# Two-pass engine programs, a shorter TensorE loop, and other cuts of the last transfers in a four-layer kernel bound by its weights

## The chip, the cores and the metric

The kernel runs on one core of a Trainium2 chip. The metric is the device time of one execution in microseconds (us). Times of single instructions and transfers come from one profiled execution, counted from the first instruction of the span.

## The reference

An image x of 16 channels, 64 by 64, passes four layers, all in float32:

```
x = L0(x, style)    # blur statistics: (x - mean(x)) / std(x) * std(style) + mean(style), 13 x 13 Gaussian
x = L1(x, weights)  # patch and window attention, below
x = L2(x, w1, b1, w2, b2)  # conv3x3, relu, conv3x3, + x
x = L3(x, weights)  # the same as L1, with weights of its own
```

L1 and L3 are the bulk. The image is cut into 64 patches of 8 x 8 x 16 = 1024 values, and into 4 windows of 32 x 32 x 16 = 16384 values:

```
fl = LN(patches); pw = softmax(q k^T)  with q, k = fl @ Wqk_p      # 1024 x 2048
pf = merge(pw @ v + dwconv(v)) @ Wout_p  with v = fl @ Wv_p        # two of 1024 x 1024
ww = softmax(q k^T) of the 4 windows, with q, k = LN(pooled) @ Wqk_w   # 1024 x 2048
wv = heads(LN(windows) @ Wv_w)                                     # 16384 x 1024
wf = merge(nondiag(ww) @ wv + dwconv(wv)) @ Wout_w                 # 1024 x 16384
out = diag(ww) * pf + wf + x
```

Wv_w and Wout_w have 64 MB each, in each of the two layers.

## The kernel before, in words

**Weights.** All weights pass through SBUF once. A *slot* is 128 partitions x 2048 values (1 MB), a *half* is 8 slots (8 MB), and the buffer `ring` holds two halves, `extra` a quarter (4 slots). SyncE issues every transfer (`load_half`, L271; `load_end`, L260). Before it overwrites slots it waits on `slots_used`, which TensorE raises by one for each slot that it has read. TensorE waits on `half_landed` before the first slot of a half. The very last half is split into six pieces, `LAST_PIECES` (L58): each is a range of columns (0 to 384 is "wide", 384 to 512 "narrow") and a range of heads, and has a semaphore of its own (L306).

**TensorE's program** (`block.tensor`). L341 to L376 compute layer L0 and turn small tables. Then one hardware loop `pe.Fori(0, 2) as L` (L378) does both attention layers with the same code: statistics, Wqk_p and Wv_p (L404, L413), Wqk_w (L421), Wout_p (L469), then a loop of 4 turns over Wv_w (L485), then a loop over Wout_w (L524). A turn of that loop is two *groups* of 8 slots: `group(L, i, g)` makes 32 matmuls (L512) into `bank[6 + g]`, ScalarE copies the bank to SBUF (`copy_group`, L653), `turn_group` transposes it (L323), and VectorE adds it to the image (`add_group`, L932). The loop runs 4 turns in the first layer and `TURNS - L` = 3 in the second. Between the layers `pe.If(L < 1)` does the two convolutions of L2.

**The tail.** The fourth turn of the second layer is written out behind the layer loop, since its second group is the half in six pieces. Its order is this:

```
group(1, TURNS - 1, 0)
last_piece(0)
turn_group(4 * TURNS - 1, 0)
last_piece(1)
```

The image is then turned into rows (8 transposes) and copied to `out_rows` by VectorE and ScalarE; the last 4 rows of each window take another way: the residual is added in PSUM by 16 small matmuls against the identity (L572, L574), between pieces. Pieces 2 to 5 follow. SyncE stores the rows in two transfers of 28 rows each (L310), the wide part of the last rows (L312) and at the end the narrow part (L314).

**The other programs.** ScalarE and VectorE are unrolled over the two layers, with small loops inside for the turns. GpSimd clears buffers and makes two products per layer. All engines run free of each other but for semaphores. `image_ready` (VectorE, L731) tells that L0 is done; SyncE waits for it before it issues the second half of the ring (L271), because L0's buffers lie there.

Of the kernel before, what the change touches and what calls it, by code (L numbers as in the profile page):

```python
# [22 lines left out]
P = 128  # L23
# [34 lines left out]
LAST_PIECES = ((0, WIDE, 0, 4), (0, WIDE, 4, 6), (0, WIDE, 6, 8), (WIDE, BANK, 0, 4), (WIDE, BANK, 4, 7), (WIDE, BANK, 7, 8))  # L58
# [61 lines left out]
def build(nc, images, blurs, const, const_low, window_gains, small, l2w, ends, halves, last, out, windows_last):  # L120
    with ExitStack() as ctx, ExitStack() as engines:
# [121 lines left out]
        LAST = WIN - 4  # L243

# [4 lines left out]
        def stores_landed(sp):  # L249
            sp.wait_ge(rows_stored, 16 * 3)  # L250
            sp.wait_ge(last_stored, 16)
# [6 lines left out]
        def _(sp):  # L258
# [50 lines left out]
            for wy in range(2):  # L309
                sp.dma_start(out[wy], out_rows[wy * WIN:wy * WIN + LAST, :]).then_inc(rows_stored, 16)  # L310
# [7 lines left out]
        def _(pe):  # L318
# [19 lines left out]
            pe.wait_ge(blurs_landed, 16)  # L338
            pe.wait_ge(images_landed, 16)
            for x8 in range(NX8):  # L340
                m = mm(bank[x8 // 4][:, x8 % 4 * P:x8 % 4 * P + P], l0_in[:, x8, :], cc("blur_y"), start=True, stop=True)  # L341
            m.then_inc(blurred_y, 1)
            pe.wait_ge(squared, 1)
            for x8 in range(NX8):
                m = mm(bank[2 + x8 // 4][:, x8 % 4 * P:x8 % 4 * P + P], l0_sq[:, x8, :], cc("blur_y"), start=True, stop=True)
            m.then_inc(blurred_y2, 1)
            pe.wait_ge(blocks_built, 1)
            for sq, img, dst in ((0, 0, 5), (1, 0, 7), (0, 1, 6), (1, 1, 0)):
                pe.wait_ge(blur_copied, 1)
                if sq:  # L350
                    pe.wait_ge(blur2_copied, 2)
                mid = l0_blur[:, sq, :].rearrange("p (x i y) -> p i x y", i=2, y=IMG)[:, img]
                field = bank[dst][:, :].rearrange("p (x y) -> p x y", y=IMG)
                mm(field, blocks_x[:, 0, :], mid, start=True, stop=False)  # L354
                mm(field[:, 0:1], blocks_x[:, 1, :], mid[:, 0:1], start=False, stop=False)
                mm(field[:, 7:8], blocks_x[:, 2, :], mid[:, 7:8], start=False, stop=False)
                mm(field[:, 0:7], blocks_x[:, 3, :], mid[:, 1:8], start=False, stop=False)
                mm(field[:, 1:8], blocks_x[:, 4, :], mid[:, 0:7], start=False, stop=True).then_inc(field_ready, 1)

            pe.wait_ge(ident_built, 2)  # L360
            for x8 in range(NX8):
                m = turn(bank[4][:, x8 * IMG:x8 * IMG + IMG], l0_in[0:IMG, x8, :], rows=IMG)
            m.then_inc(field_ready, 1)

            pe.wait_ge(const_landed, 16 * 2)
            pe.wait_ge(gains_landed, 16)
            for i in range(4):
                turn(bank[2][:, i * P:(i + 1) * P], area[0][:, i * P:(i + 1) * P])
            pe.wait_ge(small_landed, 16)  # L370
            turn(bank[3][:, 0:2 * N_SMALL], area[1][0:2 * N_SMALL, 0:P], rows=2 * N_SMALL).then_inc(vec_turned, 1)

            pe.wait_ge(l0_var, 1)
            pe.wait_ge(pads_zeroed, 1)
            pe.wait_ge(l2_landed, 16)
            mm(bank[7][:, 0:N_L2], cc("repeat", C), l2[:, :], start=True, stop=True).then_inc(l2_repeated, 1)  # L376

            with pe.Fori(0, 2) as L:  # L378

                pe.wait_ge(image_ready, L + 1)  # L380
                mm(bank[0][:, :], ones, pixels, start=True, stop=True).then_inc(sums, 1)  # L381
                pe.wait_ge(py_ready, L + 1)
                pe.wait_ge(vec_copied, 1)
                for q in range(4):
                    m = mm(bank[3][32 * q:32 * q + 32, 0:32], cc("pool"), py[:, :, :].rearrange("p y (w q) -> p q y w", q=4)[:, q],
                           start=True, stop=True)
                m.then_inc(pool_ready, 1)
                pe.wait_ge(sq_ready, L + 1)
                mm(bank[0][:, :], ones, area[1][:, :], start=True, stop=True).then_inc(var_sums, 1)  # L389
                pe.wait_ge(pooled_copied, L + 1)  # L390
                mm(bank[2][:, 0:32], ones, pooled[:, :, :, :].rearrange("p a b c -> p (a b c)"), start=True, stop=True).then_inc(pool_sums, 1)
                pe.wait_ge(sqw_ready, L + 1)
                mm(bank[1][:, :], ones, area[3][:, :], start=True, stop=True).then_inc(var_sums, 1)
                pe.wait_ge(sqp_ready, L + 1)
                mm(bank[3][:, 128:160], ones, pooled_q[:, :, :].rearrange("p a b -> p (a b)"), start=True, stop=True).then_inc(var_sums, 1)

                fl = a3(0, TOK)
                pe.wait_ge(fl_ready, L + 1)
                for s in range(S_QKP, S_VP):
                    first_there(L, s)  # L400
                    w = slot_of(s).rearrange("p (m h b d) -> p m b h d", m=2, b=2, d=P)
# [608 lines left out]
```

## Time and profile before

| | us |
|---|---|
| median of 3 runs | 747.84 |
| lowest, highest | 747.6, 748.36 |
| the profiled execution | 747.63 |
| its span, first to last instruction | 746.4 |
| TensorE busy (matmul) | 436.4 (58%) |
| VectorE busy | 91.5 (12%) |
| ScalarE busy | 38.2 (5%) |
| bytes moved | 320.45 MB, 429 GB/s on average |
| mean granted TensorE clock | 0.78 of full |

### The profile page before, as it was taken

Reading aid. Unit: us, or ns where it says so; the run is one execution under the profiler, and the core shown is the slowest. Engines: PE = TensorE matmul, PEld = TensorE weight load, DVE = VectorE, ACT = ScalarE, POOL = GpSimd, SP = SyncE. Lnnn points to the kernel's source line nnn. Section 1 sums busy time; section 2 is a strip of 40 time slices with the busy share of each in tenths; the row PEclk is TensorE's granted clock in tenths of the full one; section 3 lists DMA queues with packets and bytes.
Section 4 is the critical chain, followed back from the end, with each engine's and each line's share of the span. In section 5 each row is a group of like instructions: output and inputs, shape, how many; then the busy total and the mean of one; then the engine's idle time right before and its main releaser. Section 6 shows DMA issues by size and latency. Waiting matters only on the chain.

```text
span 746.4 us, 6667 instructions
## 1 busy us (share of the span) xinstructions
PE 436.4 (58%) x2895; PEld 129.9 (17%) x2895; DVE 91.5 (12%) x254; ACT 38.2 (5%) x80; POOL 9.3 (1%) x21
## 2 busy tenths in 40 slices
PE   7699944444445454454586989445444454544548
PEld 5333200000001111111122332000000011111113
DVE  2765200000002000000005161000000020000000
ACT  2211100000000000000001111000000000000000
POOL 2100000000000000000001000000000000000000
PEclk9689977777767777777788899876776777777779
DMA  9999999999999999999999999999999999999998
GB/s 394 447 394 436 454 415 439 436 443 418 436 446 418 439 433 443 421 432 446 418 439 436 417 434 443 446 418 432 443 432 432 432 446 418 432 443 432 432 415 347
DMA packets 7923, 320.45 MB, mean 429 GB/s; under 512 B 1049, under 2 KB 1585, under 8 KB 2153
## 3 DMA queue, kind: packets, MB, share of 16 engines
q1 hardware_dynamic: 7913, 320.31, 99.5%
q8 instruction: 7, 0.11, 0.1%
q14 instruction: 3, 0.02, 0.0%
HBM read 319.82 MB, written 0.49 MB: 429 GB/s over the span
## 4 chain that ended last, share of the span: by engine, by line
DMA 64%; PE 32%; DVE 3%; ACT 1%; issue 0%; SPq 0%; DVEq 0%; ACTq 0%
DMA ring<-halves 60%; PE bank L485 10%; PE bank L512 9%; PE bank L404 4%; DMA ring<-last 4%; PE bank L421 2%; PE bank L413 2%; PE bank L536 1%; PE bank L341 1%; PE bank L323 0%; PE bank L389 0%; DMA cst<-blurs 0%; DVE ring L722 0%; PE bank L381 0%; PE bank L354 0%
## 5 line engine op out<-in xcount | busy, mean ns | idle before, releaser
L485 PE MATMUL bank<-ring,stage 128*4 128x512 f32 x1024 | 141.4, 714 | 141.1 <-DMA ring<-halves 141.1
L512 PE MATMUL bank<-ring,wf_t 128*32 128x512 f32 x960 | 137.9, 739 | 127.3 <-DMA ring<-halves 127.3
L512 PEld LDWEIGHTS bank<-ring,wf_t 128*32 128x32 f32 x960 | 33.7, 133 | 221.1 <-DMA ring<-halves 121.0
L485 PEld LDWEIGHTS bank<-ring,stage 128*4 128x4 f32 x1024 | 27.0, 97 | 255.1 <-DMA ring<-halves 154.1
L932 DVE TENSOR_TENSOR image<-bank,image 128x32 f32 (+1 forms) x30 | 5.1, 193 | 277.6 <-PE bank L323 277.6
L897 DVE COPY wv_t<-bank 128x32 f32<-128x32 f32 x2 | 0.4, 192 | 287.1 <-PE bank L323 287.1
L323 PE MATMUL bank<-ident,area 128*128 128x128 f32 (+1 forms) x117 | 18.3, 284 | 12.3 <-ACT area L653 11.1
L653 ACT COPY area<-bank 128x512 f32<-128x512 f32 x15 | 8.8, 586 | 281.2 <-PE bank L512 281.2
L404 PE MATMUL bank<-extra,area 128*64 128x512 f32 x64 | 18.2, 734 | 3.3 <-DVE area L806 3.3
L469 PE MATMUL bank<-extra,area 128*64 128x512 f32 x64 | 17.6, 712 | 2.0 <-DVE area L871 2.0
L323 PEld LDWEIGHTS bank<-ident,area 128*128 128x128 f32 (+1 forms) x117 | 12.5, 141 | 30.9 <-ACT area L653 23.8
L641 ACT COPY stage<-area 128x64 f32 x16 | 3.9, 242 | 219.3 <-PE bank L485 206.0
L421 PE MATMUL bank<-ring,pooled_n 128*32 128x512 f32 x128 | 14.6, 595 | 0.0
L847 DVE SCALAR_TENSOR_TENSOR conv_p<-v_pad,vec,conv_p 128x636 f32<-128x636 f32 x16 | 14.1, 879 | 0.4
L413 PE MATMUL bank<-ring,area 128*64 128x512 f32 x64 | 14.1, 592 | 0.0
L404 PE MATMUL bank<-ring,area 128*64 128x512 f32 x64 | 14.1, 592 | 0.0
L556 PE MATMUL bank<-ring,wf_t 128*32 128x384 f32 (+1 forms) x128 | 7.8, 382 | 0.8 <-DMA ring<-last 0.8
L404 PEld LDWEIGHTS bank<-extra,area 128*64 128x64 f32 x64 | 5.5, 171 | 14.6 <-issue 14.6
L469 PEld LDWEIGHTS bank<-extra,area 128*64 128x64 f32 x64 | 5.4, 160 | 12.7 <-issue 12.7
L687 POOL TENSOR_TENSOR area<-area,vec 128x512 f32<-128x512 f32 x2 | 2.1, 1042 | 394.1 <-DVE area L781 394.1
L341 PE MATMUL bank<-cst,ring 128*128 128x128 f32 x16 | 3.8, 431 | 4.7 <-DMA cst<-blurs 4.7
L381 PE MATMUL bank<-image,ones 128*128 128x512 f32 x4 | 3.2, 893 | 5.4 <-DVE image L731 4.6
(208 smaller groups left out, 217.0 us busy)
## 6 DMA issues: line engine op xcount, KB each, us to landing
extra<-ends SPq DMA_DIRECT2D x4, 4096.0 KB, 16.0
ring<-halves SPq DMA_DIRECT2D x4, 4096.0 KB, 20.3
ring<-last SPq DMA_DIRECT2D x1, 3072.0 KB, 22.1
ring<-last SPq DMA_DIRECT2D x2, 1536.0 KB, 25.5
ring<-last SPq DMA_DIRECT2D x1, 1024.0 KB, 28.6
ring<-last SPq DMA_DIRECT2D x1, 768.0 KB, 29.6
ring<-halves SPq DMA_DIRECT2D x33, 29.4
ring<-images SPq DMA_DIRECT2D x1, 512.0 KB, 3.6
```

What stands on the lines that cost most here:

```text
L323: return mm(dst, src, ident[0:rows, 0:rows], start=True, stop=True, is_transpose=True)
L341: m = mm(bank[x8 // 4][:, x8 % 4 * P:x8 % 4 * P + P], l0_in[:, x8, :], cc("blur_y"), start=True, stop=True)
L404: m = mm(bank[4 + m2][b * 64:b * 64 + 64, :], fl[:, s - S_QKP, :], w[:, m2, b], start=(s == S_QKP), stop=(s == S_VP - 1))
L413: m = mm(bank[6][b * 64:b * 64 + 64, :], fl[:, kt, :], w[:, t, b], start=(kt == 0), stop=(kt == KT - 1))
L421: m = mm(bank[7][32 * j:32 * j + 32, :], pooled_n[:, s - S_QKW, :], w[:, j * BANK:(j + 1) * BANK], start=(s == S_QKW), stop=(s == S_OUTP - 1))
L469: m = mm(bank[4][f * 64:f * 64 + 64, :], a3(8, TOK)[:, h, :], w[:, t, f], start=(h == 0), stop=(h == HEADS - 1))
L485: m = mm(bank[0][32 * j:32 * j + 4, :], stage[:, k // 8, at:at + 4], w[:, j], start=False, stop=False)
L512: m = mm(bank[6 + g][32 * j:32 * j + 32, :], wf_t[:, h, :], w[:, j], start=(h == 0), stop=(h == GROUP - 1))
L536: mm(dst[0:32, :], taps_edge[:, n, dy, 0, :], rows(dy, -1), start=False, stop=False)
L556: m = mm(dst, wf_t[:, h, :], w[:, h - h0, j], start=(h == 0 and c0 == 0), stop=(h == HEADS - 1))
L653: sc.copy(area[4 + g][:, :], bank[6 + g][:, :]).then_inc(group_copied, 1)
L847: then(v.scalar_tensor_tensor(conv_p[:, 0:159, 0:4], src, wt, conv_p[:, 0:159, 0:4], ALU.mult, ALU.add))
```

## The change

Five edits, in one step:

1. The whole programs of TensorE, ScalarE and VectorE stand inside `Fori(0, 2) as visit` with `If(visit > 0)`. In pass one the branch skips the body. VectorE's body is split into two such blocks (L0 and the first layer; the second layer and the end).
2. TensorE's loop over Wout_w runs 4 turns in both layers, with `If(i + L < TURNS)` around the second group. The unrolled group and turn behind the layer loop go, so that the turn stands directly behind its group.
3. The residual is added by 4 whole matmuls (stationary 128 x 128) and no longer by 16 of 32 columns.
4. The narrow pieces of the last half take 5, 2 and 1 heads and no longer 4, 3 and 1.
5. The rows are stored by 6 transfers of 15, 13, 11, 9, 7 and 1 rows and no longer by 2 of 28.

```diff
-LAST_PIECES = (..., (WIDE, BANK, 0, 4), (WIDE, BANK, 4, 7), (WIDE, BANK, 7, 8))
+LAST_PIECES = (..., (WIDE, BANK, 0, 5), (WIDE, BANK, 5, 7), (WIDE, BANK, 7, 8))
...
+        ROW_STORES = ((0, 0, 15), (0, 15, LAST), (1, 0, 11), (1, 11, 20), (1, 20, 27), (1, 27, LAST))
...
-            for wy in range(2):
-                sp.dma_start(out[wy], out_rows[wy * WIN:wy * WIN + LAST, :]).then_inc(rows_stored, 16)
+            for wy, lo, hi in ROW_STORES:
+                sp.dma_start(out[wy, lo:hi], out_rows[wy * WIN + lo:wy * WIN + hi, :]).then_inc(rows_stored, 16)
...
+            with pe.Fori(0, 2) as visit:
+                with pe.If(visit > 0):
+                    pe.wait_ge(blurs_landed, 16)
...
+                    with pe.Fori(0, 2) as L:
...
-                with pe.Fori(0, TURNS - L) as i:
-                    for g in range(2):
-                        group(L, i, g)
-                        turn_group(i * 2 + (2 * TURNS * L + g + 1), g)
+                        with pe.Fori(0, TURNS) as i:
+                            group(L, i, 0)
+                            turn_group(i * 2 + (2 * TURNS * L + 1), 0)
+                            with pe.If(i + L < TURNS):
+                                group(L, i, 1)
+                                turn_group(i * 2 + (2 * TURNS * L + 2), 1)
...
-            group(1, TURNS - 1, 0)
             last_piece(0)
-            turn_group(4 * TURNS - 1, 0)
             last_piece(1)
...
             for s8 in range(4):
-                for j in range(4):
-                    if s8 < 3:
-                        mm(bank[7][32 * j:32 * j + 32, s8 * P:s8 * P + P], residual[:, s8, j, :], ident, start=False, stop=False)
-                    else:
-                        mm(bank[6][32 * j:32 * j + 32, 0:P], residual[:, s8, j, :], ident, start=True, stop=False)
+                dst = bank[7][:, s8 * P:s8 * P + P] if s8 < 3 else bank[6][:, 0:P]
+                mm(dst, residual[:, s8].rearrange("p j w -> p (j w)"), ident, start=(s8 == 3), stop=False)
...
+            with act.Fori(0, 2) as visit:
+                with act.If(visit > 0):
...
+            with dve.Fori(0, 2) as visit:
+                with dve.If(visit > 0):
+                    first()
+                    layer(0)
+                with dve.If(visit > 0):
+                    layer(1)
```

In VectorE's program `first()` and `layer(L)` hold the old code of L0 and of one layer, unchanged.

## Rows read from the trace of the kernel before

**Rows 1.** The page: the span, and the DMA engines' busy tenths in 40 slices:
```profile
span 746.4 us, 6667 instructions
...
DMA  9999999999999999999999999999999999999998
```

**Rows 2.** The chain of waits at the end: start us, us, what:
```profile
713.72 29.57 DMA ring<-last
```

**Rows 3.** The timeline of the tail: start us, us, engine, line [idle before]:
```profile
724.40 9.22 PE L512 MATMUL bank<-ring,wf_t 128*32 128x512 f32 x64 [9.30 <-DMA ring<-halves]
733.43 2.77 PE L556 MATMUL bank<-ring,wf_t 128*32 128x384 f32 x32
...
736.13 0.66 PE L323 MATMUL bank<-ident,area 128*128 128x128 f32 x4
...
739.16 0.86 PE L572 MATMUL bank<-ident,area 128*32 128x128 f32 x24
...
739.88 0.78 SPq L310 DMA_DIRECT2D out<-extra  x2
...
740.06 2.50 PE L556 MATMUL bank<-ring,wf_t 128*32 128x384 f32 x48
...
743.34 1.08 PE L556 MATMUL bank<-ring,wf_t 128*32 128x128 f32 x32 [0.79 <-DMA ring<-last]
744.49 0.29 DVE L953 COPY area<-bank 128x128 f32<-128x128 f32 x1 [4.97 <-PE bank L556]
744.81 0.36 SPq L314 DMA_DIRECT2D windows_last<-area  x1
```

**Rows 4.** Packets that begin in 34.3 to 35.0 us, then in 36.1 to 36.2:
```profile
DMA packets 30, 0.98 MB, mean 1404 GB/s; under 512 B 15, under 2 KB 15, under 8 KB 15
...
DMA packets 2, 0.07 MB, mean 655 GB/s; under 512 B 1, under 2 KB 1, under 8 KB 1
```

**Rows 5.** Packets in 403.3:404.1, in 721.5:722.2, in 722.7:723.5, in 723.75:723.82 us:
```profile
DMA packets 12, 0.39 MB, mean 492 GB/s; under 512 B 6, under 2 KB 6, under 8 KB 6
...
DMA packets 18, 0.22 MB, mean 316 GB/s; under 512 B 9, under 2 KB 9, under 8 KB 9
...
DMA packets 20, 0.34 MB, mean 430 GB/s; under 512 B 6, under 2 KB 6, under 8 KB 6
...
DMA packets 5, 0.10 MB, mean 1404 GB/s; under 512 B 1, under 2 KB 1, under 8 KB 1
```

**Rows 6.** Instruction packets in 31:265, in 265:731, in 731:746.4 us (packets, MB, share):
```profile
q8 instruction: 5, 0.08, 0.1%
q14 instruction: 1, 0.01, 0.0%
...
q14 instruction: 2, 0.02, 0.0%
...
q8 instruction: 2, 0.03, 1.0%
```

**Rows 7.** The timeline of the start, three of its lines:
```profile
4.74 3.78 PE L341 MATMUL bank<-cst,ring 128*128 128x128 f32 x16 [4.74 <-DMA cst<-blurs]
...
27.09 1.06 DVE L731 TENSOR_TENSOR image<-ring,bank 128x512 f32<-128x512 f32 x1
...
28.17 0.35 SPq L271 DMA_DIRECT2D ring<-halves  x1
```

**Rows 8.** The list of waits: total us, times, longest:
```profile
PE bank L323 <- ACT area L653: 11.1, 14, 0.8
```

**Rows 9.** Busy time by stretch; the granted clock is the figure behind POOL:
```profile
381.00:404.90 23.90, 18.66 (x92) 5.48 (x85) 5.41 (x13) 1.91 (x3) 1.04 (x1) 0.99 1.02 440
724.40:729.16 4.76, 4.76 (x27) 1.32 (x30) 0.00 (x0) 0.00 (x0) 0.00 (x0) 0.54 0.98 418
```

**Rows 10.** L524's loop branches (min, median, max ns), and L345 in the timeline:
```profile
L524 PEldq COMPARE_BRANCH  x7: 76/208/222, 270.2 to 714.8; - x7
...
8.31 2.07 PE L345 MATMUL bank<-cst,ring 128*128 128x128 f32 x16
```

More of the change, by code:

```diff
@@ L335, in first_there @@
                     half_there(L, None, s // HALF)
[L338 to L371, printed above, removed]
@@ L723, in _, with first @@
[L723 to L732 removed]
+            def first():
+                dve.wait_ge(images_landed, 16)
+                v.tensor_tensor(l0_sq[:, :, :], l0_in[:, :, :], l0_in[:, :, :], ALU.mult).then_inc(squared, 1)
+                dve.wait_ge(blurs_landed, 16)
+                v.tensor_tensor(blocks_x[:, :, :].rearrange("p b (x c) -> p (b x) c", c=C), cc("taps_x").unsqueeze(2).to_broadcast([P, 5 * XM, C]),
+                                cc("same_c").unsqueeze(1).to_broadcast([P, 5 * XM, C]), ALU.mult).then_inc(blocks_built, 1)
+                dve.wait_ge(blurred_y2, 1)
+                v.tensor_copy(l0_blur[:, 1, BANK:2 * BANK], bank[3][:, :]).then_inc(blur2_copied, 1)
+                mean_c = area[6][:, :]
+                dve.wait_ge(mean_sq, 1)
+                then(v.tensor_copy(mean_c, bank[5][:, :]))
+                for i, (sq, fields) in enumerate(((7, 2), (0, 4))):
+                    dve.wait_ge(field_ready, fields)
+                    dve.wait_ge(mean_sq, i + 1)
+                    then(v.tensor_tensor(l0_part[:, i], bank[sq][:, :], l0_part[:, i], ALU.subtract))
+                    v.tensor_scalar(l0_part[:, i], l0_part[:, i], 0.0, None, ALU.max).then_inc(l0_var, 1)
+                    if i == 0:
+                        dve.wait_ge(l0_std, 1)
+                        then(v.tensor_scalar(l0_part[:, 0], l0_part[:, 0], EPS, None, ALU.add))
+                        then(v.reciprocal(l0_part[:, 0], l0_part[:, 0]))
+                work = l0_blur[:, 0, 0:BANK]
+                dve.wait_ge(field_ready, 5)
+                then(v.tensor_tensor(work, bank[4][:, :], mean_c, ALU.subtract))
+                then(v.tensor_tensor(work, work, l0_part[:, 0], ALU.mult))
+                dve.wait_ge(l0_std, 2)
+                then(v.scalar_tensor_tensor(work, l0_part[:, 1], EPS, work, ALU.add, ALU.mult))
+                dve.wait_ge(pads_zeroed, 1)
+                v.tensor_tensor(pixels.rearrange("p y x -> p x y"), work.rearrange("p (x y) -> p x y", y=IMG),
+                                bank[6][:, :].rearrange("p (x y) -> p x y", y=IMG), ALU.add).then_inc(image_ready, 1)
@@ L766, in softmax, with layer @@
                 return v.tensor_tensor(x, x, wide(2), ALU.mult)
-            for L in range(2):
+            def layer(L):
                 vv = vec[:, L, :]
```

508 lines of the change are left out of this document (255 added, 253 removed).

## The prediction

> **What bounds the kernel now.** The page comes first: 16 DMA engines are busy in every slice, so the transfers run without a gap [rows 1]. The chain of waits says where the span ends: a weight transfer of 29.57 us hands over at 743.34 us [rows 2]. The timeline of the tail then shows TensorE starting its last full group at 724.40 when a half lands, working almost without a break, standing idle once, for 0.79 us at 743.34, and finishing at 744.42; a 0.29 us copy and the store at 744.81 follow, and the span ends at 746.4 [rows 3]. So two things run side by side in the last 20 us: the stream of weights and a chain of TensorE work that has only 0.79 us of play.
>
> What I looked for next is why a half lands when it does. Each transfer leaves one small closing packet (under 512 B) per engine. The first half closes on 15 engines inside 34.3 to 35.0 us and on the sixteenth at 36.1, 1.1 to 1.8 us behind [rows 4]. The half that TensorE waits for at 724.40 closes on 9 engines inside 721.5 to 722.2, on 6 between 722.7 and 723.5, and on one at about 723.8; at 403.3 to 404.1, 6 engines were late [rows 5]. These counts match the instruction fetches: queue 8 (TensorE, since it is active when TensorE enters new code) five and queue 14 one by 265 us, which makes 6 late engines; two more on queue 14 by 731 us [rows 6], which make 7, so that one of them fell on an engine that was late already. A fetch pushes its engine back, and that is never made good, because the stream has no gap. The engine hit twice from queue 14 sets the landing, 723.8; the engines hit once closed by 723.5, the unhit ones by 722.2.
>
> **Part 1, the pass that only jumps.** Each of the three programs runs its loop twice; the first time every branch skips the body, so the sequencer goes to its end and back. What this can buy is that instruction blocks of the end are fetched at about 1 to 2 us, when the first work of TensorE still waits for data, until 4.74 us [rows 7], and not in the middle of the stream. VectorE and ScalarE are short: all three queue 14 fetches should move to the start. VectorE has two skipped blocks, so its pass also touches its middle. TensorE's queue 8 fetches stay for all that lies between the first block and the last: the four early ones of [rows 6]. The last block, and the one after it, move to the start. For the landing this removes the doubly late engine and leaves the once late ones: 723.8 (723.79 by the closing packet) becomes about 723.45, **-0.34 us** for the start of the tail and for each last piece. The bounds are 0 (nothing moves, or an early fetch falls on an engine that is hit again) and -1.7 us (all fetches early: 723.8 to 722.1 at best).
>
> That blocks stay once fetched is what the trace bears out: TensorE's layer loop runs all its code again from 400 us on, and queue 8 shows no packet between 265 and 731 us [rows 6]. The Trainium skill says otherwise ("Runtime: NRT & Kernel Launch", section "Instruction fetch mechanics"): the instruction memory has room for only two blocks, prefetch is purely sequential, and a taken branch to a block outside that window stalls for its fetch. By that rule pass one would gain nothing, since the end block would be dropped again; for TensorE the trace disagrees, with its zero packets over a whole second pass, and for VectorE and ScalarE, which never jump back so far, nothing here shows it.
>
> The cost of the jumps lies at the start. TensorE, VectorE and ScalarE begin 2 to 4 us later at worst (two or three fetches in a row, and the two packets of queue 8 behind 731 us took 1.0% of 16 engines' 15.4 us, 1.2 us each [rows 6]). What hides it is the queue: image_ready comes with the end of L731 at 28.15 and releases the second half at 28.17 [rows 7], while the first half still streams until 34.4 [rows 4]; from the issue of the last store to the end of its packets pass 1.6 us (744.81 to 746.4), so the cover is at least 34.4 - 28.2 - 1.6 = 4.6 us. If the cover is gone, every us beyond it lengthens the run by 1 us. I take 0.
>
> **Part 2, the shorter TensorE loop.** The last half group (group 14, counted from 0, of the second layer) goes back into the loop and is no longer unrolled behind it: 128 instructions (64 matmuls and 64 loads) and a turn less in the program, the same executed. But its order changes. Before, last_piece(0), 2.70 us, stood between the group and its turn and hid the copy by ScalarE. Now the turn follows at once and TensorE waits for the copy: 11.1 us over 14 such waits is **+0.79 us** [rows 8]. Behind the waiting turn all pieces, the row turns and the residual are queued. Then come the branches: the new If taken, the ends of both loops, the If of the convolution and the outer loop's end, five of about 0.21 us [rows 10]; they are 1.05 us beside a turn of 0.66 us, so **+0.3 us** (bounds 0 and 1.05). In all earlier turns the new If lies in the time in which TensorE waits for a half (9.30 us before 724.40) and costs nothing.
>
> **Part 3, the residual** becomes 4 whole matmuls of 128 x 128 instead of 16 of 32 columns. The 16 took 0.90 us (739.16 to 740.06) because four of them run side by side [rows 3]. Eight whole matmuls of 128 x 128 x 128 took 2.07 us at full clock [rows 10], so four take 1.04: **+0.14 us**; below, the four turns of 0.66 us [rows 3] bound it at -0.24.
>
> **Part 4, the clock.** The tail starts at the low clock, granted 0.54 on average from 724.40 to 729.16, then 1.0 [rows 9]. A start 0.34 us earlier with the same rise spends 0.34 us more at half speed: **+0.17 us**.
>
> **Part 5, heads 5, 2, 1.** Of the narrow pieces, the last two wait together today: 32 matmuls in 1.08 us from 743.34. With 5, 2, 1 only 24 of them (0.81 us) would follow that landing, a gain of 0.27 us where the stream decides. Here TensorE decides, so the same work comes in another order: 0.
>
> **Part 6, six row stores.** SyncE took 0.78 us for two stores, so six take 2.3 us [rows 3]. They begin near 740.8 and end near 743.1, with the wide store behind them; that store is not waited for before the narrow one, which comes at 744.8 or later. Hidden; gone is the cover only if the rows come 1.5 us later still. The same 56 rows are moved, behind all loads. 0.
>
> **The sum.** TensorE's chain: -0.34 (start) +0.79 (copy) +0.3 (branches) +0.14 (residual) +0.17 (clock) -0.79 (the idle time that it eats up) = +0.27 us. The stream's own end: the last piece 0.34 us earlier, and 0.27 us saved by its shape, so about -0.5 us; the later of the two counts. The profiled run took 747.63 us around its span of 746.4, so it becomes 747.9; the median of the runs lies 0.21 us above the profiled one, which gives **748.1 us**. About 0.2%, or 1.5 us, is what a measurement of this kernel can tell from no change: 746.34 to 749.34 counts as the same.
>
> **The rivals.** (a) *The stream still decides*: copy and branches are covered, or the clock rises earlier. For it: the once idle 0.79 us; against it: nothing stands between group and turn any more. 747.84 - 0.5 = 747.3 us. Chance 0.20. (b) *All fetches move to the start*, TensorE's middle ones too. For it: the pass touches all programs; against it: TensorE's pass jumps over its middle. The tail starts 1.7 us earlier at 722.7, and the sum becomes -1.7 +0.79 +0.3 +0.14 +0.17 to 0.85 -0.79, so -1.1 to -0.4, 746.7 to 747.4; with branches and residual at their lower bounds 746.1. Chance 0.17, of which 0.12 faster by over 0.2%. (c) *The jump does not do what it says*: the early blocks are dropped and fetched again, and the late engine stays at 723.8. That is the rule of the skill named above; by rows it costs the 0.34 and gives back the 0.17: 748.3 us. Chance 0.15. (d) *Slower: the clock falls in the new gap.* The 0.8 us wait at 733.3 has 11 us of TensorE work behind it, and if the granted clock drops to 0.5 there for one more stretch like the first (4.8 us), half of that, 2.4 us, is added: 750.5 us. It decides from the point at which the grant falls before 744. Against it: the stretch from 381 us, which holds waits of the same length, was granted 0.99 [rows 9]. Chance 0.06. (e) *Slower at the start:* the jumps take more than the 4.6 us of cover, say 7: 750.5 us. Chance 0.04. The forecast keeps 0.38.
>
> **How the numbers follow.** The likeliest case spans 747.3 to 748.9 (branches and residual at their bounds, the clock's rise some us earlier or later). The range takes in (a), (c) and most of (b), and part of the slower ones: 746.4 to 749.3. Faster by over 0.2%: 0.14. Slower: (d) and (e), 0.10. Same: 0.76.
>
> **What would show it.** Part 1: the queue 14 packets of the span stand before 5 us, queue 8 has four in mid-stream and none behind 731; the half that starts the tail closes on no engine later than the once hit ones. Part 2: a wait of 0.8 us for ScalarE's copy between group and turn, and the first piece 0.2 to 0.4 us behind the turn. Part 3: four matmuls in 0.7 to 1.04 us. Part 5: no idle time of TensorE before the last pieces. Wrong it is if TensorE still idles for the stream at the end, if the last landing moves by more than 0.5 us, or if the second half is issued behind 33 us.

## The result and the profile after

| | before | after |
|---|---|---|
| median of 16 runs, us | 747.81 | 749.29 |
| lowest run | 747.5 | 747.78 |
| highest run (one disturbed run of before left out) | 748.36 | 750.58 |
| the profiled execution | 747.63 | 748.88 |
| its span | 746.4 | 747.6 |

The changed kernel is slower: the ratio is 1.002 with the interval 1.0012 to 1.0027, and the medians differ by +1.48 us. I had forecast +0.26. The changed kernel also scatters more, over 2.8 us where before spans 0.9 in these 16 runs. In the three sets of runs beside the experiments, the kernel before spans 1.0, 1.0 and 2.5 us, the last with a single run at 750.03.

The profiled execution shows +1.25 us of it, so that is what can be followed line by line. The first view is the timeline of the tail of the changed kernel (start us, us, engine, line, what, [idle before]); it answers to [rows 3].

```profile
725.59 8.47 PE L515 MATMUL bank<-ring,wf_t 128*32 128x512 f32 x64 [8.31 <-DMA ring<-halves]
...
734.13 0.58 ACT L655 COPY area<-bank 128x512 f32<-128x512 f32 x1 [17.56 <-PE bank L515]
...
734.77 0.66 PE L324 MATMUL bank<-ident,area 128*128 128x128 f32 x4 [0.72 <-ACT area L655]
...
736.15 4.08 PE L561 MATMUL bank<-ring,wf_t 128*32 128x384 f32 x48 [0.73 <-issue]
...
741.09 1.06 PE L574 MATMUL bank<-ident,area 128*128 128x128 f32 x8
...
742.08 3.58 PE L561 MATMUL bank<-ring,wf_t 128*32 128x384 f32 x80
...
745.73 0.29 DVE L958 COPY area<-bank 128x128 f32<-128x128 f32 x1 [4.19 <-PE bank L561]
746.04 0.35 SPq L315 DMA_DIRECT2D windows_last<-area  x1
```

The tail starts at 725.59 and not at 724.40: +1.19 us. From there to the end of the last matmul it takes 20.07 us (725.59 to 742.08 + 3.58 = 745.66), before 20.02 us (724.40 to 744.42). So the whole loss of this execution stands ahead of the tail, and inside the tail the gains and losses cancel out.

What delays the start is seen in the closing packets. These are counts of packets of the changed kernel in 722.1 to 722.8, in 723.6 to 724.25 and in 725.05 to 725.1 us; they answer to the last three lines of [rows 5].

```profile
DMA packets 15, 0.24 MB, mean 339 GB/s; under 512 B 7, under 2 KB 7, under 8 KB 7
...
DMA packets 21, 0.32 MB, mean 492 GB/s; under 512 B 8, under 2 KB 8, under 8 KB 8
...
DMA packets 5, 0.10 MB, mean 1966 GB/s; under 512 B 1, under 2 KB 1, under 8 KB 1
```

Seven DMA engines close early, eight are late, and one closes at 725.07, 2.90 us behind the first (722.17). Before, nine were early, six late, and the last came at 723.79, 2.20 us behind the first (721.60). The landing is 1.28 us later. Of that, 0.70 is a wider spread, and 0.57 is that even the first engine closes later. Most of this is there 35 us into the run already. These are the closing packets of the very first half in the changed kernel, counted in 34.8 to 35.4, 36.2 to 36.7 and 37.7 to 37.8 us; they answer to [rows 4].

```profile
DMA packets 24, 0.80 MB, mean 1338 GB/s; under 512 B 11, under 2 KB 11, under 8 KB 11
...
DMA packets 8, 0.26 MB, mean 524 GB/s; under 512 B 4, under 2 KB 4, under 8 KB 4
...
DMA packets 3, 0.13 MB, mean 1311 GB/s; under 512 B 1, under 2 KB 1, under 8 KB 1
```

The first engine closes at 34.88 (before 34.38), the last at 37.73, 2.85 us behind it (before 1.77 behind). From there to the tail the largest distance stays between 2.79 and 2.91 us: the fetches of the middle set other engines back, none of them as far.

The instruction packets say where the late engines come from. Stretches of the changed kernel: 0 to 12, 12 to 265.5, then 731 to 747.6 us (between 265.5 and 731 there is none), against [rows 6].

```profile
q8 instruction: 2, 0.03, 1.0%
q14 instruction: 3, 0.02, 0.5%
...
q8 instruction: 5, 0.08, 0.1%
...
q8 instruction: 1, 0.02, 0.4%
```

The three fetches of queue 14 (VectorE and ScalarE) did move out of the middle. But TensorE's five are still there, at 35, 69, 83, 115 and 265 us (before 32, 66, 81, 112 and 264), and two more are made at the start. And "the start" is not 1 to 2 us: the five early fetches begin at 3.65, 3.76, 3.94, 10.37 and 10.60 us, when the weight transfers run already. In all, ten fetches lie in the stream ahead of the tail's half where there were eight.

The start itself, TensorE's taken branch and the start of its work, then the issue of the second half; they answer to [rows 7]. The first line is the listing of one source line (min, median, max ns of two branches, when), the others are of the timeline.

```profile
L340 PEldq COMPARE_BRANCH  x2: 77/2618/5159, 1.1 to 6.9; - x2
...
3.63 1.58 SPq L267 DMA_DIRECT2D cst<-const_low  x1
...
7.11 3.76 PE L344 MATMUL bank<-cst,ring 128*128 128x128 f32 x16 [7.11 <-DMA cst<-blurs]
...
29.78 1.05 DVE L735 TENSOR_TENSOR image<-ring,bank 128x512 f32<-128x512 f32 x1
...
30.86 0.35 SPq L272 DMA_DIRECT2D ring<-halves  x1
```

One branch to code that is not there took 5.16 us. TensorE's first matmul comes at 7.11 and not at 4.74, the image at 30.83 and not at 28.15, and the second half is issued at 30.86 and not at 28.17 us. The first half still streams then: its first engine is done at 34.88, the last at 37.73. So this 2.7 us stays hidden. The closing packets bear that out, since from the first half to the next the first engine needs 19.36 us (34.88 to 54.24), and before it needed 19.35 (34.38 to 53.73).

### The profile page after: what moved, and what is told of

It reads as the page before. It is cut to its first block, busy times and chain, and to the rows that moved or that the text cites. A ratio compares the mean times of both kernels' runs of the same rounds, so it can differ in the third digit from the quotient of the medians.

```text
span 747.6 us, 6658 instructions
## 1 busy us (share of the span) xinstructions
PE 436.8 (58%) x2871; PEld 130.1 (17%) x2871; DVE 90.8 (12%) x254; ACT 38.1 (5%) x80; POOL 9.3 (1%) x21
## 4 chain that ended last, share of the span: by engine, by line
DMA 60%; PE 35%; DVE 4%; issue 1%; ACT 1%; SPq 0%; DVEq 0%; ACTq 0%
DMA ring<-halves 59%; PE bank L515 10%; PE bank L488 10%; PE bank L407 4%; PE bank L416 2%; PE bank L424 1%; PE bank L472 1%; PE bank L561 1%; PE bank L541 1%; PE bank L324 1%; DVE conv_p L851 1%; DMA cst<-blurs 1%; PE bank L392 1%; PE bank L344 1%; DVE ring L726 0%
## 5 line engine op out<-in xcount | busy, mean ns | idle before, releaser
L488 PE MATMUL bank<-ring,stage 128*4 128x512 f32 x1024 | 143.0, 721 | 141.2 <-DMA ring<-halves 141.2
L392 PE MATMUL bank<-area,ones 128*128 128x512 f32 x4 | 4.1, 1140 | 4.3 <-ACT area L609 4.3
```

The costliest lines, as they stand in the source:

```text
L488: m = mm(bank[0][32 * j:32 * j + 4, :], stage[:, k // 8, at:at + 4], w[:, j], start=False, stop=False)
```

## The experiments

Three theories are set against each other. The *stream theory*: the pass costs time because its instruction fetches fall into the running weight stream and push DMA engines back. Its two rivals are the *tail theory*, that the new order of the tail (copy wait, branches) costs it; and the *start theory*, that the later start of the engines reaches the end. All comparisons are against the kernel before on the same chip, whose median was 747.7 to 747.8 us each time.

**The change without the pass.**

```diff
-            with pe.Fori(0, 2) as visit:
-                with pe.If(visit > 0):
+            if True:
+                if True:
```

(and so in ScalarE's and VectorE's programs)

> The changed kernel with the jumping pass taken out of all three programs; loop, residual, narrow pieces and row stores stay changed. Theory F (the instruction fetches that the pass causes fall into the stream of weights and push DMA engines back): the half that starts the tail lands near 723.8 us as before the change, TensorE starts its last group near 724.4 and not 725.6, and the median falls back to 747.8 to 748.0 us. Rival T (the new order of the tail, with TensorE waiting 0.7 us for the copy and 0.7 us behind the turn, makes the kernel slower): the median stays at 749.0 to 749.3 us.

Measured: 748.02 us (747.54 to 748.5), ratio 1.0004 (0.9995 to 1.0013). The slowdown is gone. Its tail in the timeline:

```profile
724.40 9.05 PE L515 MATMUL bank<-ring,wf_t 128*32 128x512 f32 x64 [9.42 <-DMA ring<-halves]
734.17 0.66 PE L324 MATMUL bank<-ident,area 128*128 128x128 f32 x4 [0.72 <-ACT area L655]
735.32 4.08 PE L561 MATMUL bank<-ring,wf_t 128*32 128x384 f32 x48 [0.49 <-issue]
...
741.24 3.25 PE L561 MATMUL bank<-ring,wf_t 128*32 128x384 f32 x80
```

It starts at 724.40, as before, and ends at 744.49 (before 744.42), with the copy wait of 0.72 us and no idle time for the stream. So everything but the pass is worth about +0.25 us by the medians, which can't be told from nothing. The tail theory, which asked for 749.0 or more, falls.

**The pass alone**, put into the kernel before.

```diff
+            with pe.Fori(0, 2) as visit:
+                with pe.If(visit > 0):
```

(the same for ScalarE, and the two blocks for VectorE; nothing else)

> The kernel before with the jumping pass alone, in all three programs; nothing else changed. Theory F: queue 14 carries its three packets and queue 8 two packets within 3.5 to 11 us, the closing packets of a half spread over about 2.9 us and not 2.2, TensorE starts the tail 1.2 us later, and since its chain there is as long as before, the median is 748.8 to 749.2 us. Rival T: 747.7 to 747.9 us.

Measured: 748.99 us (748.3 to 750.18), ratio 1.0017 (1.0008 to 1.0026), +1.22 us. With the +0.25 of the kernel without the pass that makes +1.47, and the whole change has +1.48: the two parts add up. Its instruction packets in 0 to 12, 12 to 265.5 and 731 to 747.7 us:

```profile
q8 instruction: 2, 0.03, 1.0%
q14 instruction: 3, 0.02, 0.5%
...
q8 instruction: 5, 0.08, 0.1%
...
q8 instruction: 2, 0.03, 0.8%
```

TensorE fetches all seven blocks that it fetched before, at the same places of the program, and two in addition. For TensorE the pass moves nothing. Its tail:

```profile
744.66 1.08 PE L559 MATMUL bank<-ring,wf_t 128*32 128x128 f32 x32 [0.80 <-DMA ring<-last]
```

TensorE still waits 0.80 us for the last piece, as in [rows 3], but the piece lands later: the stream's end has moved with the rest. The half that starts the tail closes between 722.06 and 725.11 us, 3.04 apart.

**The pass in VectorE and ScalarE only, and in TensorE only.** Each is the kernel with the pass alone, with the pass taken out again of some programs; for the first:

```diff
-            with pe.Fori(0, 2) as visit:
-                with pe.If(visit > 0):
+            if True:
+                if True:
```

For the second the same is done to ScalarE and VectorE, and TensorE keeps it.

> The kernel before with the jumping pass in VectorE's and ScalarE's programs only. Theory F with the fetches of queue 14 and queue 8 adding up only where they meet on an engine: queue 14 carries nothing between 12 and 746 us, queue 8 stays as before (five by 265 us), no fetch meets another, so the closing packets of a half spread over about 1.9 us, the tail starts 0.2 to 0.3 us earlier and the median is 747.4 to 747.7 us. Rival (an early fetch costs an engine as much as a late one and falls on one that is hit again): the spread is 2.2 us or more, 747.8 to 748.6 us.

Measured: 748.2 us (747.91 to 748.29), ratio 1.0002 (0.9993 to 1.0011); the medians differ by +0.43. Three fetches at 3.7 to 10 us, none of queue 14 later: these moved, and the time did not get better. First and last close of the tail's half: 721.79 and 724.28 (2.50 apart). My expectation (1.9 apart, 747.4 to 747.7 us) failed, and the numbers are those of its rival: an early fetch costs as much as a late one.

> The kernel before with the jumping pass in TensorE's program only. Theory F: two more packets of queue 8 within 3.5 to 11 us, the five of the middle stay, none of them saved but the one near 731 us; TensorE's first matmul comes at about 7 us. If two packets of queue 8 meet on one engine the spread is 2.9 us or more and the median 748.7 to 749.4 us; if they do not, the doubly late engine of queue 14 (2.2 us) still decides and the median is 747.8 to 748.1 us.

Measured: 748.61 us (747.67 to 750.06), ratio 1.001 (1.0 to 1.0019), +0.84. Two fetches more, and none saved: the one near 731 us, which I had expected to go, is there at 731.78. First and last close are 722.11 and 724.14. The two parts of the pass make +1.27 together, the whole pass +1.22. TensorE's part has two thirds of it by the medians, but neither part alone stands clear of noise: both intervals touch or hold 1.

**The pass before the first load.** This run was meant to tell the stream theory from the start theory. SyncE waits until all three programs are back from pass one, and only then issues the first transfer, so the early fetches meet an empty queue.

```diff
+            sp.wait_ge(awake, 3)
+            first_loads(sp)
...
             with pe.Fori(0, 2) as visit:
                 with pe.If(visit > 0):
+                    pe.sem_inc(awake, 1)
```

(and so for ScalarE and VectorE)

> The kernel before with the jumping pass in all three programs, and SyncE issues its first transfer only when all three have come back from it (a count of three on a semaphore). Theory F (a fetch costs the stream only because it stands between the weights on a DMA engine): the early fetches now meet an idle queue, so the pass is over sooner than the 6.3 us of TensorE's branch, and the closing packets of a half spread over about 1.9 us (the five later packets of queue 8 alone), not 3.0. The stream starts 2 to 5 us later, so the median is 749.5 to 752.5 us. Rival (the spread comes from something else in the two-pass program, its back jumps or the delayed first work): the spread stays near 3 us and the median is 751 to 754 us.

Measured: 753.88 us (752.15 to 754.96, 5 runs), ratio 1.0086 (1.0073 to 1.01). This is outside the 749.5 to 752.5 that the stream theory had asked for and inside the rival's 751 to 754; the spread of the profiled run speaks the other way. Its instruction packets between 2.0 and 5.41 us (no data packet begins there), and SyncE's first issue in the timeline:

```profile
q8 instruction: 2, 0.03, 3.6%
q14 instruction: 3, 0.02, 2.1%
...
5.41 0.39 SPq L248 DMA_DIRECT2D ring<-images  x1
```

Even with an idle queue the pass lasts until about 5.3 us (TensorE's taken branch took 3.30 us here, and 5.16 beside the stream): its fetches begin at 2.02 to 2.17 us, and one more of each queue at 5.13 and 5.40, when the programs have come back. All are over by 6.1 us, and the first data packet begins at 6.46. The first transfer is issued 4.60 us later than before (5.41 against 0.81). The half that starts the tail then closes like this; packets in 726.2 to 726.8 and in 727.7 to 728.2 us:

```profile
DMA packets 22, 0.27 MB, mean 451 GB/s; under 512 B 11, under 2 KB 11, under 8 KB 11
...
DMA packets 12, 0.17 MB, mean 344 GB/s; under 512 B 5, under 2 KB 5, under 8 KB 5
```

Eleven engines are early and five late, and five is the number of TensorE's fetches that remain in the stream. First and last close are 726.24 and 728.18. With the 4.60 us taken off they are 721.64 and 723.58, +0.04 and -0.21 us against before, where the pass inside the stream has +0.47 and +1.31. (The first transfer of weights moved by 4.77 us, 6.50 against 1.73; by that both figures are 0.17 lower.) So in this execution the same fetches cost nothing at the landing once they are out of the stream. The -0.21 is no gain that could be told from scatter.

The run does not separate the start theory from it. TensorE's first matmul comes at 9.40, 2.94 us behind the first data packet, as before (2.90) and not as in the changed kernel (5.28): moving the pass ahead of the loads has taken away the late start as well. What speaks against the start theory is the changed kernel itself: its stream has lost nothing to the late issue of the second half (19.36 us from close to close), while its first engine was 0.50 us late one half earlier. At the end this run waits twice for the stream:

```profile
745.90 1.08 PE L562 MATMUL bank<-ring,wf_t 128*32 128x128 f32 x32 [0.60 <-DMA ring<-last]
747.76 1.08 PE L562 MATMUL bank<-ring,wf_t 128*32 128x128 f32 x32 [0.78 <-DMA ring<-last]
```

What this run leaves open weighs as much: its median. 753.88 is 6.1 us over before, 1.5 us more than the 4.60 by which the loads start later, and that is as much as the pass costs inside the stream (+1.22). The profiled run is the fastest of the five (752.15, 4.5 us over before's profiled run); the others took 753.6 to 754.96. In them the pass may have taken longer, or the landing was worse; no trace of them exists. So that a pass outside the stream is free is shown by one trace and not by the medians.

**The other parts, one at a time**, each put into the kernel before.

The loop (edit 2, TensorE's part as in the diff of the change):

```diff
-                        with pe.Fori(0, TURNS - L) as i:
...
+                        with pe.Fori(0, TURNS) as i:
+                            group(L, i, 0)
+                            turn_group(i * 2 + (2 * TURNS * L + 1), 0)
+                            with pe.If(i + L < TURNS):
...
-            group(1, TURNS - 1, 0)
             last_piece(0)
-            turn_group(4 * TURNS - 1, 0)
```

> The kernel before with the loop edit alone: the last group and its turn stand in the loop, nothing else changed. My prediction of the blind part: TensorE waits 0.7 to 0.8 us for the copy, the first piece begins 0.3 us behind the turn, and of the 0.79 us of idle time before the last pieces nothing is left, so the span ends 0.2 to 0.4 us later, 748.0 to 748.2 us. By the profile of the changed kernel the gap behind the turn is 0.73 us, which gives 0.6 to 0.8 us, 748.4 to 748.6 us. Rival: all of it is covered, 747.8 us.

Measured: 747.97 us (747.42 to 749.45), ratio 1.0004 (0.9995 to 1.0013). The profiled run was one of its long ones (748.97), and is worth a look for that:

```profile
725.57 9.12 PE L515 MATMUL bank<-ring,wf_t 128*32 128x512 f32 x64 [9.35 <-DMA ring<-halves]
735.40 0.66 PE L324 MATMUL bank<-ident,area 128*128 128x128 f32 x4 [0.72 <-ACT area L658]
736.56 4.08 PE L561 MATMUL bank<-ring,wf_t 128*32 128x384 f32 x48 [0.51 <-issue]
```

The copy wait is 0.72 again and the gap behind the turn 0.51. Its tail starts at 725.57 without any pass: here the last engine closed 3.01 us behind the first (725.06), nearly as in the changed kernel (2.90, 725.07). An engine was 2.42 us behind at the first half already, with a single fetch so far, and the fetch of queue 14 at 438.86 set back another that was late: one engine was 2.15 behind before it and 2.86 after, 3.01 at the tail. A landing as late as the changed kernel's thus comes without a pass too, in a kernel whose median can't be told from before's.

The residual (edit 3):

```diff
-                        mm(bank[7][32 * j:32 * j + 32, s8 * P:s8 * P + P], residual[:, s8, j, :], ident, start=False, stop=False)
...
+                mm(dst, residual[:, s8].rearrange("p j w -> p (j w)"), ident, start=(s8 == 3), stop=False)
```

> The kernel before with the residual in 4 whole matmuls alone. Prediction: they take 1.0 to 1.1 us from the first to the next piece against 0.90 for the 16 small ones, and the time stays the same, since TensorE idles 0.79 us behind it: 747.8 us, at most 0.1 off. Rival (fewer instructions are quicker): 0.6 to 0.7 us, and the time also stays.

Measured: 747.92 us (747.5 to 748.33), ratio 1.0 (0.9991 to 1.0009). The four whole matmuls stand in a group of eight (the trace has two records for each of these float32 matmuls) from 739.86, and the next group begins at 740.85, so they take 0.99 us where the 16 small ones took 0.90:

```profile
739.86 1.06 PE L574 MATMUL bank<-ident,area 128*128 128x128 f32 x8
...
740.85 2.37 PE L559 MATMUL bank<-ring,wf_t 128*32 128x384 f32 x48
```

The narrow pieces (edit 4):

```diff
-LAST_PIECES = (..., (WIDE, BANK, 0, 4), (WIDE, BANK, 4, 7), (WIDE, BANK, 7, 8))
+LAST_PIECES = (..., (WIDE, BANK, 0, 5), (WIDE, BANK, 5, 7), (WIDE, BANK, 7, 8))
```

> The kernel before with narrow pieces of 5, 2 and 1 heads alone. Prediction: TensorE waits for the last landing but one as before, and 24 small matmuls follow it and not 32, so the span ends 0.1 to 0.27 us earlier: 747.5 to 747.7 us. Rival (the last piece lands too late for that, so TensorE waits for it and the shape brings nothing): 747.8 us.

Measured: 747.73 us (747.53 to 748.87), ratio 0.9999 (0.999 to 1.0008). Its profiled run is a long one too (748.87), for another reason. In it, no engine closed the very first half between 34.3 and 35.3 us, where fifteen did before [rows 4]; eleven did between 35.3 and 36.0:

```profile
DMA packets 3, 0.20 MB, mean 197 GB/s; under 512 B 0, under 2 KB 0, under 8 KB 0
...
DMA packets 22, 0.72 MB, mean 1030 GB/s; under 512 B 11, under 2 KB 11, under 8 KB 11
```

So its whole stream was 1.04 us late from the start on (first close 35.42 against 34.38), with no pass in the kernel, and its spread at the tail is no wider than 1.84 us. The medians with and without this edit are 0.06 us apart, which can't be told from nothing.

The six row stores (edit 5):

```diff
-            for wy in range(2):
-                sp.dma_start(out[wy], out_rows[wy * WIN:wy * WIN + LAST, :]).then_inc(rows_stored, 16)
+            for wy, lo, hi in ROW_STORES:
+                sp.dma_start(out[wy, lo:hi], out_rows[wy * WIN + lo:wy * WIN + hi, :]).then_inc(rows_stored, 16)
```

> The kernel before with nothing but the six row stores in place of five or fewer. The stores are issued by SP's queue while TensorE still works on the last product, so every theory says 747.8 us, within 0.3 of the kernel before, and the interval of the ratio holds 1. If the additional issue (0.07 to 0.35 us of a store's issue by the rows) fell on the path, it would be 748.0 or more; if shorter stores let the last one land earlier, 747.6. The landing of the half that starts the tail should again scatter by 1.9 to 3.0 us from first to last engine, with the same ten instruction fetches as before.

(The kernel before has two row stores.) Measured: 747.61 us (747.56 to 748.1), ratio 0.9999 (0.999 to 1.0009). The six issues lie where they were expected, SyncE is done with the wide store at 741.9, and 2.7 us remain before the last:

```profile
739.35 2.17 SPq L311 DMA_DIRECT2D out<-extra  x6
741.58 0.35 SPq L313 DMA_DIRECT2D windows_last<-area  x1
744.64 0.36 SPq L315 DMA_DIRECT2D windows_last<-area  x1
```

**The runs side by side.** For each profiled run: fetches in the stream ahead of the tail's half (queue 8 and queue 14), the time of SyncE's issue of `const_low` (at 3.6 us, in the first kernel at 8.3), the engines that closed that half late (0.9 us or more behind the first), the first close, the last, and their distance. There is one profile for each kernel.

| kernel | fetches | issue | late engines | first | last | spread |
|---|---|---|---|---|---|---|
| pass before the first load | 5 + 0 | 0.43 | 5 | 726.24 | 728.18 | 1.94 |
| before | 5 + 3 | 0.44 | 7 | 721.60 | 723.79 | 2.20 |
| without the pass | 5 + 3 | 0.43 | 7 | 721.53 | 723.88 | 2.35 |
| stores alone | 5 + 3 | 0.44 | 7 | 721.55 | 723.62 | 2.07 |
| residual alone | 5 + 3 | 0.83 | 7 | 721.49 | 724.10 | 2.61 |
| loop alone | 5 + 3 | 1.43 | 7 | 722.06 | 725.06 | 3.01 |
| narrow pieces alone | 5 + 3 | 1.20 | 10 | 722.75 | 724.59 | 1.84 |
| pass in VectorE, ScalarE | 5 + 3 | 0.53 | 7 | 721.79 | 724.28 | 2.50 |
| pass in TensorE | 7 + 3 | 1.37 | 10 | 722.11 | 724.14 | 2.03 |
| pass alone | 7 + 3 | 1.56 | 9 | 722.06 | 725.11 | 3.04 |
| after | 7 + 3 | 1.58 | 9 | 722.17 | 725.07 | 2.90 |

What is shown most directly is that a fetch sets one engine back for the rest of the run, since each can be watched in the trace before. At the half of 402.18 us six engines are late, by 1.21, 1.61, 1.74, 1.77, 1.79 and 1.86 us. Queue 14 fetches 8 KB at 413.06. At the half of 421.53 the 1.21 is gone and one engine closes 2.17 behind the first, and it is 2.20 behind at the tail. These are the closing packets of 423.6 to 423.8 us:

```profile
DMA packets 2, 0.03 MB, mean 164 GB/s; under 512 B 1, under 2 KB 1, under 8 KB 1
```

So the reading on which Part 1 rests holds: one engine was hit twice by queue 14, and it sets the landing. A single fetch of TensorE (16 KB) leaves its engine 1.61 to 1.94 us behind the first (the five of the first row), or about 1.5 us behind the others.

What the table does not show is that ten fetches give a wider spread than eight. With eight it runs from 1.84 to 3.01 us, with ten from 2.03 to 3.04, and the narrow pieces alone have ten late engines with eight fetches. Nor does the first close go by the fetches alone: it is 722.06 or later in the five kernels in which the issue of `const_low` took 1.20 us or more, and at most 721.79 in the others (in the first row with the 4.60 us taken off). Three of the five have TensorE's pass inside the stream, and two have no pass at all.

## Why the prediction was wrong

**What failed is Part 1**, its -0.34 us for the start of the tail, and with it the 0 that I took for the price of the jumps. In the profiled run the start came 1.19 us later, and the pass alone costs +1.22 us by the medians. Three assumptions stand behind the two terms.

*That the fetches come at 1 to 2 us.* I had taken the time at which the branch is issued (1.1 us) for the time of the fetch. The packets begin at 3.65 to 3.94 us, and one more for each of the two queues at 10.4 and 10.6, when TensorE is in pass two already. The first data packet begins at 1.83 us, so the early fetches are in the stream as much as the old ones. The delays stay for the rest of the run in either case: the early place buys nothing. In the one trace with the fetches ahead of the stream the same blocks cost nothing at the landing.

*That TensorE's blocks at the end, fetched by the pass, are not fetched again.* I forecast four fetches in mid-stream and none behind 731 us. The profile has five and one. The one that vanished, at 731 us, is gone in the kernel without the pass too, so the shorter program removed it (the loop edit alone has it gone as well). The pass alone repeats all seven fetches of before, with two on top. For TensorE this is rival (c), to which I gave 0.15. I had argued against it from the layer loop, which runs twice without a fetch from 265 to 731 us [rows 6]. That row shows that blocks survive a loop in which they are used again; it does not show that one survives while the rest of the program is loaded over it, and this one does not: two blocks come at the start, five follow in mid-stream as before, and none of the old ones is spared, the last at 741 us included. The rule of the Trainium skill ("Runtime: NRT & Kernel Launch", "Instruction fetch mechanics") that a taken branch to a block which is not there stalls for its fetch agrees with the 5.16 us of this branch; its rule that only two blocks are held does not explain the zero packets between 265.5 and 731 us, here as before. (The same section also gives TensorE 128 KiB, which would be eight blocks of 16 KB; no run here counts them.) For VectorE and ScalarE the forecast was right in the main: no packet of queue 14 comes behind 11 us, though the third comes at 10.60 and not before 5.

*That a pass costs nothing while the start is covered.* The cover did hold: the second half is issued at 30.86 us, below the 33 that I had named as the limit, and rival (e) did not come. But I had counted the price of the jumps only as time of the three engines, not as two transfers of 16 KB on the DMA engines that carry the weights. I had myself read that "a fetch pushes its engine back, and that is never made good", and then applied it to the fetches that go and not to those that come. What should have stood in the sum is a price for five fetches at the start of the stream, two of them of 16 KB that come on top. How large, the runs give only as a whole: +1.22 us for the pass by the medians. The +1.28 of the landing in the profiled run (0.70 in the spread, 0.57 in the first close) can't be put down to the two fetches alone, since the loop alone lands as late without them. Of my own signs of being wrong one came: the last landing moved by more than 0.5 us.

The start of the tail has +1.19 instead of -0.34, 1.53 us more than forecast. The other steps below gave back 0.61 (clock -0.92, branches +0.43, copy and residual -0.12), which leaves +0.92 over the +0.27: +1.19.

**Part 2, the copy wait**: forecast 0.79, measured 0.72 in three kernels. Right within 0.07. **The branches**: forecast 0.3, bounds 0 to 1.05; measured 0.49 without the pass, 0.51 in the loop alone, 0.73 with it. The chosen value was 0.2 too low in two of the kernels and 0.43 in the changed one; the full 1.05 would have been further off in the first two. Why the same branches took 0.24 us longer with the pass is open.

**Part 3, the residual**: forecast +0.14, measured +0.09 (0.99 against 0.90).

**Part 4, the clock**: forecast +0.17 for an earlier start; the start came later, and the group at the head of the tail took 8.47 us and not 9.22, so -0.75. The granted clock (the figure behind POOL) before, then in the changed kernel:

```profile
724.40:728.77 4.37, 4.37 (x24) 1.23 (x28) 0.00 (x0) 0.00 (x0) 0.00 (x0) 0.50 0.97 416
728.77:733.60 4.83, 4.83 (x52) 1.55 (x48) 0.00 (x0) 0.00 (x0) 0.00 (x0) 1.00 0.99 416
...
725.59:728.45 2.86, 2.86 (x16) 0.79 (x20) 0.00 (x0) 0.00 (x0) 0.00 (x0) 0.50 1.02 438
728.45:734.06 5.61, 5.60 (x52) 1.32 (x44) 0.00 (x0) 0.00 (x0) 0.00 (x0) 1.00 0.98 416
```

The clock rises to its high level (2.4 GHz, granted 1.00) at 728.77 us before and at 728.45 here; [rows 9] with its mean of 0.54 had made me take the end of its stretch, 729.16, for the rise. The low level lasted 2.86 us of work and not 4.37, and half of the difference is the measured 0.75. The pricing of Part 4 holds in all eleven profiles: the group takes 7.02 to 7.04 us and half of its time at the low level. But the rise does not keep its place. In the ten kernels whose loads start at the usual time it lies between 727.90 and 730.56 us, and the group takes 8.47 to 9.84; what sets it I can't say. So 0.60 of the 0.75 is the later start, and the rest, an earlier rise, is chance.

**Part 5 and 6**: forecast 0 and 0, measured 747.73 and 747.61 against 747.79 and 747.73. No difference can be told, as forecast.

**The sum**, from the profiled runs: start +1.19, group -0.75, copy +0.72, branches +0.73, residual +0.09, idle time eaten up -0.79, which is +1.19; measured +1.24 at the last matmul and +1.25 for the execution, so 0.05 is not assigned. The chain of the tail is as the forecast had it, TensorE works without idle time for the stream at the end, and rival (a) is out; what moved is the point it hangs on. The remaining 0.23 us to the +1.48 of the medians lies within the scatter of single runs.

**The range** (746.4 to 749.3) just holds the 749.29, and that is luck: the step at its head went the other way. The chances of "slower" lay on two mechanisms that did not come, 0.10 together, and rival (c), the nearest, had only the gain gone and not a loss in its place. The row that spoke for it was on my table: the count of fetches.

Not settled: why the engines that no fetch hits close 0.47 to 0.57 us later where TensorE's pass runs inside the stream. In the changed kernel it is there in the first half already (34.88 against 34.38) and stays between 0.50 and 0.59, and it is absent (+0.04) in the run with the pass ahead of the loads. It goes with a long issue by SyncE at the start. These are the issues of `const_low` before, in the loop alone and in the narrow pieces alone:

```profile
3.56 0.44 SPq L266 DMA_DIRECT2D cst<-const_low  x1
...
3.71 1.43 SPq L267 DMA_DIRECT2D cst<-const_low  x1
...
3.56 1.20 SPq L267 DMA_DIRECT2D cst<-const_low  x1
```

In the last two the first half's first close is 0.24 and 1.04 us late, with no pass in the kernel. So a slow start of the stream happens without the pass. That the pass makes it more likely would fit the medians and the three profiles that have it, but with one profile for each kernel it isn't shown, and neither is how the +1.22 us divides between the fetches and such a start.

## What to carry to other kernels

Where transfers without a gap set the time, an instruction fetch is a transfer as well. Count the instruction packets before and after an edit, see on how many engines they fall, and price each one that lies in the stream, wherever it lies, at what it sets its engine back. Code fetched ahead can help only if the fetch is over before the first data packet and the block is still there when it is needed (even then no gain was shown here); read both from the times of the packets, not from the place of the branch. When a kernel waits for the last of 16 engines, look at the closing packets first, those of the first transfer as well, and take more than one profile: eight fetches gave spreads of 1.84 to 3.01 us here, so one trace of each kernel does not tell eight fetches from ten.

## What the runs showed of the hardware that I had not expected

- A taken branch to code that was not loaded took 5.16 us beside the stream; its fetch packet began 2.7 us after the branch (1.1 to 3.76). With an idle queue the branch took 3.30 us, its packet began at 2.07, and all programs were back from the jump by 5.4 us.
- An instruction packet of 16 KB took 1.02 to 1.11 us on its queue in the middle of the stream, but its engine fell about 1.5 us behind the others; one of 8 KB took 0.31 to 0.33 us and left its engine some 0.65 to 0.97 us behind. In the trace before, neither was made good by the tail, up to 690 us later.
- ScalarE and VectorE keep the code that pass one brought (no fetch behind 11 us); TensorE fetches two blocks more at 3.76 and 10.37 us and no block less later.
- In the trace before, the first engine closes a half of 8 MB every 19.35 or 19.36 us from 102 to 373 us, so that a difference of 1 us at the tail could be followed back to the first 35 us of a run. It is not always so: in the loop alone the first engine lost 0.37 us near 430 us (421.77 to 431.85, before 421.53 to 431.24).
- The group at the head of the tail took 7.02 to 7.04 us and half of its time at the low clock in all eleven profiles.
